# Expert slots of a mixture-of-experts layer: from one-hot matmuls to indirect writes into a table in memory

## The reference

```
x = layernorm(x + self_attention(x))              # 16 heads, low-rank latents, rotary part, causal
x = layernorm(x + cross_attention(x, ctx) @ W.T + b)   # 16 heads
p = softmax(x @ Wg + bg)                          # 8 experts
top2, weights = top_k(p, 2) renormalised to 1
y = sum over the 2 chosen experts e: weight_e * (gelu(x @ W1[e] + b1[e]) @ W2[e] + b2[e])
out = layernorm(x + y)
```

## Time and profile before

| | us |
|---|---|
| median of 3 runs | 707.59 (707.23 to 709.61) |
| span of the profiled execution (the page gives no other time of its own for it) | 704.8 |
| PE busy | 610.6 (87%) |
| DVE busy | 517.4 (73%) |
| ACT busy | 397.3 (56%) |
| POOL busy | 292.9 (42%) |

### The profile page before, as it was taken

The page is one execution under the profiler, slowest core; times in us unless marked ns, Lnnn a source line. Parts: engine busy times, 40 slices in busy tenths (PEclk is TensorE's granted clock), DMA queues, the critical chain, the costliest instruction groups (busy, mean ns, idle before and its releaser), DMA issues.

```text
span 704.8 us, 22698 instructions
## 1 busy us (share of the span) xinstructions
PE 610.6 (87%) x8063; PEld 447.7 (64%) x8064; DVE 517.4 (73%) x1106; ACT 397.3 (56%) x847; POOL 292.9 (42%) x245
## 2 busy tenths in 40 slices
PE   2678989999999999999886797899999999999940
PEld 1456756676676667667564556678777777777720
DVE  5797898997786878677677986867666666666635
ACT  4335668767568484866778693554434444444414
POOL 3688574436264641543111012233444444444422
PEclk9789999999999999999999997999999999999985
DMA  8435253240322304304344045122222222222226
GB/s 276 151 103 151 78 166 91 63 121 6 111 69 72 82 1 119 110 21 118 106 121 136 1 119 180 19 32 46 47 47 45 45 45 45 44 45 39 43 40 223
DMA packets 39839, 59.45 MB, mean 84 GB/s; under 512 B 6768, under 2 KB 27504, under 8 KB 39632
## 3 DMA queue, kind: packets, MB, share of 16 engines
q1 hardware_dynamic: 32272, 48.12, 23.3%
q0 software_dynamic: 7488, 10.23, 8.9%
HBM read 34.08 MB, written 11.67 MB: 65 GB/s over the span
## 4 chain that ended last, share of the span: by engine, by line
PE 34%; DVE 11%; DMA 6%; ACT 4%; issue 4%; POOL 2%; ACTq 1%; SPq 1%; DVEq 1%; POOLq 0%
PE bank L1688 6%; PE bank L1690 3%; DVE mxc L1085 3%; DMA x_sb<-x_rows,slot_row 2%; PE scores L1678 2%; PE bank L1678 2%; PE scores L1680 2%; PE scores L1679 2%; PE bank L1292 2%; DMA acc_rows<-x,slot_row 2%; PE bank L1680 2%; PE bank L1679 2%; POOL acc_rows L627 1%; ACT probs L742 1%; PE scores L1343 1%
## 5 line engine op out<-in xcount | busy, mean ns | idle before, releaser
L742 ACT ACTIVATE probs<-scores 128x768 f32<-128x768 f32 (+1 forms) x128 | 114.3, 918 | 51.0 <-PE scores L1349 40.2
L627 POOL DMA_INDIRECT acc_rows<-x,slot_row x39 | 65.2, 1671 | 132.7 <-DVE x L1198 129.8
L1688 PE MATMUL bank<-w_sb,wp 128*128 x312 | 109.9, 380 | 1.9 <-DVE wp L1185 1.9
L1085 DVE TENSOR_REDUCE mxc<-scores 128x4 f32<-128x1024 f32 x64 | 76.5, 1217 | 20.4 <-PE scores L1363 19.8
L1690 PE MATMUL bank<-w_sb,wp 128*128 x312 | 85.1, 273 | 0.0
L813 ACT ACTIVATE probs<-scores,b_sb 128x128 f32<-128x128 f32 x160 | 45.5, 368 | 63.3 <-PE scores L1680 63.3
L813 ACT ACTIVATE probs<-bank,b_sb 128x128 f32<-128x128 f32 x152 | 43.4, 370 | 65.6 <-PE bank L1680 65.6
L1183 DVE CAST wp<-probs 128x512 f16<-128x512 f32 x78 | 36.1, 462 | 60.3 <-ACT probs L813 59.8
L1050 DVE TENSOR_REDUCE mx<-scores 128x6 f32<-128x768 f32 x64 | 59.8, 950 | 15.7 <-PE scores L1331 15.2
L1678 PE MATMUL scores<-xT,w_sb 128*128 128x128 f16 x320 | 61.2, 223 | 2.2 <-DVE xT L909 1.2
L1679 PE MATMUL scores<-xT,w_sb 128*128 128x128 f16 x320 | 61.2, 223 | 0.0
(11 more groups left out here) (267 smaller groups left out, 1712.1 us busy)
## 6 DMA issues: line engine op xcount, KB each, us to landing
w_sb<-w_sb SPq DMA_DIRECT2D x192, 64.0 KB, 2.4
wstage<-in_w_exp SPq DMA_DIRECT2D x16, 512.0 KB
w_sb<-in_w_exp SPq DMA_DIRECT2D x8, 512.0 KB, 5.3
wp<-in_w_exp SPq DMA_DIRECT2D x8, 512.0 KB, 4.2
x_sb<-in_x_by_feature SPq DMA_DIRECT2D x8, 256.0 KB, 3.5
ctx_raw<-in_ctx SPq DMA_DIRECT2D x8, 256.0 KB, 3.1
x_res<-in_x SPq DMA_DIRECT2D x8, 256.0 KB, 3.5
x_rows<-x SPq DMA_DIRECT2D x8, 256.0 KB, 3.1
```

Of the source, the lines that this page charges most:

```text
L627: nc.gpsimd.indirect_dma_start(out=acc_rows[:, :], out_offset=bass.IndirectOffsetOnAxis(ap=slot_row[:, n:n + 1], axis=0), in_=yb[n % 2], i ...
L742: nc.scalar.activation(probs[:, 2 * (k % 4):2 * (k % 4) + 2, 0:cols], ps_p[pair[u, k, b]][:, :, 0:cols], ACT.Exp, scale=(SELF_SCALE, CROSS ...
L1085: nc.vector.tensor_reduce(mxc[:, 2 * k:2 * k + 2, :], ps_p[pair[u, k, b]][:, :, :].rearrange("p h (a k) -> p h a k", a=2), axis=AX.X, op=A ...
L1688: mm(o[:, 0:2 * D], ah[:, u, f, :], weights(e, at, 2 * D), start=(f == 0), stop=(f == FC - 1), skip_group_check=True)
```

## The change

The one-hot matrices and their matmuls are gone. A table in memory (`slot_table`, 16384 rows of 2 floats, 8 bytes each; row = 2048 * expert + rank) is filled with zeros at the start by SP. `gate_slots` on DVE computes the row number and casts it to an integer. For each block of 128 tokens and each of the two choices POOL issues one indirect DMA that writes 128 entries of 8 bytes (`put_slot`): 20 for the first group, 12 for the late one. When all have landed POOL loads the whole table back, 128 KB, in one DMA (`load_slots`), and `gate_table` reads that. DVE's `gate_late_tiles` stands in three parts behind tiles 1, 2 and 3, where it was one block behind tile 4.

```diff
 GPSIMD_ORDER
-cr.5 cx.7 sr.7 ss.7 ke.7 cr.6 gg.4 cr.7
+cr.5 cx.7 sr.7 ss.7 gp0.4 gp1.4 gp2.4 ke.7 cr.6 gp3.4 gp4.4 gl.4 gg.4 cr.7
...
+                        sp.dma_start(slot_table_rows, oP[0][:, 0, :]).then_inc(z_st, 16)
...
+            def put_slot(t, c):
+                nc.gpsimd.indirect_dma_start(
+                    out=slot_table[:, :], out_offset=bass.IndirectOffsetOnAxis(ap=slot_at[:, c, t:t + 1], axis=0),
+                    in_=slot_entry[:, t, c, :], in_offset=None).then_inc(t_st, 16)
+
+            def load_slots(g, t1):
+                pool.wait_ge(t_st, 32 * t1)
+                nc.gpsimd.dma_start(slots_seen[g].rearrange("p l a -> p (l a)"), slot_table_rows).then_inc(t_ld[g], 16)
...
+                elif u == "gate_put":
+                    if k == 0:
+                        pool.wait_ge(z_st, 48)
+                        pool.wait_ge(v_key, 1)
+                    for t in (2 * k, 2 * k + 1):
+                        for c in range(2):
+                            put_slot(t, c)
+                elif u == "gate_load":
+                    pool.wait_ge(a_cv, B)
+                    pool.wait_ge(p_cl, B)
+                    load_slots(0, SEEN * TT)
...
                 if n and n + AHEAD - 1 < N_TILES:
                     gather(n + AHEAD - 1)
+                if n == 0:
+                    pool.wait_ge(v_key, 2)
+                for t in range(3 * n, 3 * n + 3):
+                    if t < 2 * (NT - SEEN * TT):
+                        put_slot(SEEN * TT + t // 2, t % 2)
+                if n == 4:
+                    load_slots(1, NT)
                 scatter(n)
...
 def gate_slots
-                link(nc.vector.tensor_scalar(exps[:, at, :], rank, 1.0 / P, 0.5 / P - 0.5, ALU.mult, ALU.add))
-                link(nc.vector.tensor_scalar(exps[:, at, :], exps[:, at, :], 1.5 * 2.0 ** 23, None, ALU.add))
...
+                link(nc.vector.tensor_tensor(exps[:, at, :], rank, tab[:, C_EROW:C_EROW + E].unsqueeze(1).broadcast_to([P, n, E]), ALU.add))
+                link(nc.vector.tensor_tensor(picked[:, :, at, :], onehot[:, :, at, :],
+                                             exps[:, at, :].unsqueeze(1).broadcast_to([P, 2, n, E]), ALU.mult))
+                link(nc.vector.tensor_reduce(rs1[:, 0:2, at], picked[:, :, at, :], axis=AX.X, op=ALU.add))
+                nc.vector.tensor_copy(slot_at[:, :, at], rs1[:, 0:2, at]).then_inc(v_key, 1)
...
-            def gate_table(g, slots, i0, i1):
-                pe.wait_ge(v_S, SEEN + g)
+            def gate_table(g, i0, i1):
+                pe.wait_ge(t_ld[g], 16)
                 pe.wait_ge(v_sel, g + 1)
```

More of the change, by code:

```diff
@@ L59 @@
 C_EP = C_DUMMY + 1
-C_E16 = C_EP + E
-C_RP = C_E16 + E
+C_EROW = C_EP + E
+C_RP = C_EROW + E
 C_ALL = C_RP + 1
@@ L210, in decoder_layer @@
 def decoder_layer(nc, x, ctx_in, w_kv, g_kv, w_q, wq_content, wq_rope, wk_content, wk_rope, wv, wo, wx,
-                  x_by_feature, xb, wg, bg, w_exp, b1t, b2, table, masks, out, x2_rows, acc_rows):
+                  x_by_feature, xb, wg, bg, w_exp, b1t, b2, table, masks, out, x2_rows, acc_rows, slot_table):
     stack = ExitStack()
@@ L315, in decoder_layer @@
         onehot, picked = [xT_flat[1][:, i * 2 * NT * E:(i + 1) * 2 * NT * E].rearrange("p (k t e) -> p k t e", k=2, e=E) for i in range(2)]
[L316 to L319, removed]
+        slot_entry = swaps[:, 0:4 * NT].rearrange("p (t c a) -> p t c a", c=2, a=2)
+        slot_at = swaps[:, 4 * NT:6 * NT].bitcast(I32).rearrange("p (c t) -> p c t", c=2)
+        slots_seen = [ctx_raw[:, i, :].rearrange("p (l a) -> p l a", a=2) for i in range(2)]
         flat = oT[:, :, :].rearrange("p c t -> p (c t)")
@@ L662, in gate_exp @@
                 nc.scalar.activation(exps[:, t0:t1, :], shift[:, t0:t1, :], ACT.Exp).then_inc(a_re, 1)
[L664 to L671, removed]
             done = Counter()
@@ L950, in gate_slots @@
[L950 to L959, removed]
@@ L1383, in gate_ranks @@
                 last.then_inc(pe_rank, 1)
-            def gate_scatter(g, t, first, last=None):
-                pe.wait_ge(a_oh, t + 1)
-                for c in range(2):
-                    mm(ps_slots[g], oh_lane[:, t % 2, c, :], oh_vals[:, t % 2, c, :, :].rearrange("p a l -> p (a l)"),
-                       start=(t == first and c == 0), stop=(t == (last or first + 1) and c == 1)).then_inc(pe_slot, 1)
-            def gate_table(g, slots, i0, i1):
-                pe.wait_ge(v_S, SEEN + g)
+            def gate_table(g, i0, i1):
+                pe.wait_ge(t_ld[g], 16)
                 pe.wait_ge(v_sel, g + 1)
                 for i in range(2):
-                    last = mm(ps_fin[g][:, i * (i1 - i0):(i + 1) * (i1 - i0)], slots_of(slots, i), slot_t[2][:, i0:i1], start=True, stop=True)
+                    last = mm(ps_fin[g][:, i * (i1 - i0):(i + 1) * (i1 - i0)], slots_seen[g][:, :, i], slot_t[2][:, i0:i1], start=True, stop=True)
                 last.then_inc(pe_fin, 1)
-            def slots_of(slots, i):
-                return slots[:, i * P:(i + 1) * P]
             at, covered = Counter(), {}
@@ L1457, in bank3_free @@
                 once(v_key, at["gate_ranks"])
-                once(v_S, at["gate_scatter"])
                 once(v_lg, at["logits"])
@@ L1479, in _ @@
                     bank1_free()
-                    once(t_ld, 32)
+                    once(tab_ld, 32)
                     pe.wait_ge(v_kvn, b + 1)
@@ L1740, in _ @@
                     gate_ranks(*GATE[1])
-                elif n in (2, 3, 4):
-                    for t in range(GATE[1][1] + 2 * (n - 2), GATE[1][1] + 2 * (n - 1)):
-                        gate_scatter(1, t, GATE[1][1], NT - 1)
                 elif n == 6:
-                    gate_table(1, slots_all, FIRST, N_TILES)
+                    gate_table(1, FIRST, N_TILES)
             with pe.Fori(0, (N_TILES - 2 - FIRST) // 2) as j:
```

114 lines of the change are left out of this document (41 added, 73 removed), and 4 rows, old and new, of the table UNITS.

## The result

The changed kernel takes 727.31 us, median of 4 runs (726.4 to 731.04), against 708.3 of the kernel before: ratio 1.0286 [1.0249, 1.0323]. Its profiled span is 724.9 us against 704.8, that is +20.1. Forecast were 707.6 and a range up to 723.

What follows compares the result with a forecast made beforehand. It took the chain at the end of attention and, in the expert phase, PE with POOL's gather queue behind it as bounds; 4.2 - 1.2 - 3.2 + 0.2 = 0.0 left the span at 704.8, forecast 707.6 us, range 701 to 723.

Steps and rivals of the forecast that it cites:

- The puts on POOL: POOL's indirect writes of table entries: 1.4 us each with the gap, bounds 1.25 and 1.93.
- Dear puts: Rival: a put costs as much as the accumulating scatter, 1.63 + 0.30 to issue; 723.5 us, slower; chance 0.23.
- puts held by DVE: Rival: DVE's five weight pieces each hold a put under way, table 6 us late; 713.6 us, slower; chance 0.12.
- The rule on the shared port pair: A DMA issued from GpSimd waits until DVE's instruction ends; by the rows 0.2 us a put.
- The +3.3 us up to the selection: End of attention: PE's table selection starts at 426.3 instead of 423.01, behind puts, landing and load.
- 12 puts and then keep: POOL, first group: 12 puts from 389.5 end at 406.3; keep and root follow, waiting for nothing.
- Last put to load: End of attention: the last put, issued at 419.3, lands 3.4 us later, at 422.7; bounds 2.8 and 4.4.
- The clock: PE idle some 7 us before the selection, so low clock: projection takes twice 1.97 us, selection 0.4 more; +1.9 us.
- One-hots removed in attention: 40 records of PE matmuls and 20 comparisons go, ahead of the table selection; counted as nothing.
- the -1.2 for the wait: Expert phase: late gate_slots halves and PE's 1.20 us wait for DVE's xT at 447.91 goes; -1.2 us.
- the -1.0 for the clock: Tile 0: the low clock stretch begins earlier and may end before the tile does; between 0 and -2.7 us.
- -3.2 for slots 3 to 8: Expert phase: one-hot matmuls go, POOL gets three puts an iteration; 33.2 us from slots 3 to 8 against 36.45.

Runs made afterwards that it cites:

- f3: Changed kernel with its 32 indirect stores made plain, to consecutive rows, and its two loads reading a constant table: ratio 0.9916 to the kernel before.
- h1: Changed kernel with plain stores in attention (20), indirect ones in the expert phase (12), loads reading a constant table: ratio 1.0039.
- b3: Kernel before plus 8-byte indirect stores that nobody needs, 6 and 4 in two runs at the end of attention: ratio 1.0163.
- c2: Changed kernel with each store waiting until the last but one before it has landed, at most two under way: 739.2 us, ratio 1.0481.
- h2: Kernel before plus 20 indirect 8-byte stores, one in each of tiles 13 to 32 behind the gather, nobody waiting: ratio 1.0085.
- f2: Kernel before with its 39 gathers and 39 scatters as plain loads and stores, the scatters' adding left out: ratio 0.9961.
- d3: Kernel before plus 12 indirect 8-byte stores in the expert phase, three behind each of gathers 3 to 6, nobody waiting: ratio 1.0139.
- the run with gathers: Kernel before plus 20 indirect gathers of 8 bytes at the changed kernel's store places, results unused: ratio 1.0266.
- b1: Kernel before plus 20 indirect 8-byte stores, one at a time between other POOL operations from batch 2 to batch 5 of attention: ratio 1.0234.

## Why the prediction was wrong

**The puts on POOL.** Right, and a little cheap: 1.26 to 1.48 us from start to start within a run, mostly 1.27 (1.4 taken). "Dear puts" (from 1.6 us a put on) is out, and so is "puts held by DVE": none of 32 took over 1.174 us. The rule on the shared port pair (the Trainium skill, SBUF — State Buffer, SBUF: two separate sides) would have shown as longer puts; the longest is 0.2 us over the median.

**The step that failed** is the assumption under every term: that a put costs what POOL spends on it, and what queues behind it. I counted POOL's row and not what a call does to the others. Of the rivals the price of "dear puts" (723.5 us) came closest, by another mechanism; that is luck. The +3.3 us up to the selection became +17.9:
- 12 puts and then keep: predicted at 406.3, was 413.18, **+6.9**. I wrote that keep waits for nothing; it waited 7.43 us for batch 6's residual. In f3, with plain puts and a granted clock as low as here (0.53 and 0.50 between 395 and 405 us; 0.50 in the changed kernel, 1.00 in the trace of before), keep came at 407.12. So 6.1 us go with the index, that is with PE's late completions (6.2 us at 406.29 in the changed kernel). The other 0.8 are there in f3 as well, where the projection of batch 6 takes 3.55 us at the low clock.
- keep, root and 8 puts: 12.4 us against 13.0 predicted, **-0.6**.
- Last put to load: 3.4 predicted, 11.8 measured, **+8.4**. The bounds of 2.8 and 4.4 came from gathers alone in their stretch. In f3, with plain puts, the load waited 4.45 us for the landing instead of 10.86.
- Load to selection: 3.55 against 3.4 and 0.1 to start, 0.

**The clock.** Right in kind and near in size: from the selection to tile 0 it took 12.8 us against 11.3, +1.4; predicted were +1.9, and -1.0 in tile 0 itself, behind its first matmul. The projection took 3.76 us instead of 1.97, and the windows after show a granted clock of 0.50 (1.2 GHz) where PE had waited 6.39 us for the table:

```profile
435.00:440.00 5.00, 0.00 (x0) 0.00 (x0) 0.00 (x0) 1.24 (x2) 0.59 (x1) 0.59 0.86 195
440.00:445.00 5.00, 4.06 (x12) 3.46 (x13) 1.38 (x3) 1.06 (x1) 2.20 (x2) 0.50 0.16 32
```

**One-hots removed in attention: nothing.** Right as far as f3 shows: tile 0 at 435.13 without them, 434.34 with them.

**Expert phase.** From tile 0 to slots 3 the -1.2 for the wait and the -1.0 for the clock were -1.8 together. But -3.2 for slots 3 to 8 was +3.6. With plain stores it is -6.3, so the gain from the removed one-hots was there and larger than I said, and 12 indexed calls turn it round (h1, 40.6 us). I had forecast that POOL's iterations would be the bound, 7.4 us without idle time. They were not:

```profile
477.88 1.60 POOL L648 DMA_INDIRECT acc_rows<-x,slot_row  x1 [2.67 <-DVE x L1186]
...
485.14 1.60 POOL L648 DMA_INDIRECT acc_rows<-x,slot_row  x1 [0.30 <-issue]
...
496.98 1.60 POOL L648 DMA_INDIRECT acc_rows<-x,slot_row  x1 [4.85 <-DVE x L1186]
```

Between these scatters lie 7.3 and 11.8 us, and POOL waits for DVE, that is for tiles which the same lateness holds up. The row of waits from 455 to 510 us (us in total, times, longest) shows it on ACT, which has no such wait in the trace of before:

```profile
ACT probs L829 <- remote: 17.8, 4, 6.4
```

**The whole.** f3 at 0.9916, h1 at 1.0039, the changed kernel at 1.0286: of the 26 us between f3 and the changed kernel about 9 belong to the 12 late calls and 17 to the 20 in attention. The sum that I made would have erred by 6 us for stores without an index, and it erred by 20 for these.

**What stays open.** What in an indexed call holds back PE's completions and other queues' landings. Excluded, at the end of attention, are bytes, direction, number of rows, scattered places and POOL's time; the reading of the index by POOL and what the DMA engines do with it were not told apart. The loss has two forms, and what links them is not shown: PE's signals come late beside runs of twelve and eight calls back to back and beside three an iteration; landings come late beside fewer calls too (b3, c2), and they cost time without any late signal. That calls cost little in the steady loop (h2, f2) fits a lateness that only hurts where an engine stands waiting for a signal, as in attention with its short hand-overs between PE, DVE and ACT; but h2's 6 us lie between that and a price for each, and its calls stand one to a tile where d3's stand three to a tile, so that the wider spacing can be the reason as well: this is argued and not shown. No version here beats both kernels and computes the same: f3's gain needs stores that know their rows beforehand.

## What to carry to other kernels

Price an added transfer by what it does to the others, not by its row on the engine that issues it: add a few copies of it that nobody waits for to the old kernel and time that. It costs one run and would have settled this change. Here an indirect DMA more cost the whole kernel 0.6 to 1.2 us in a stretch with tight hand-overs between engines, with 16 rows as with 128, and 0.3 in a steady loop at one to a tile, while plain DMAs from POOL cost at most 0.1; so make few indexed calls, and keep them out of such stretches. A wait of "remote", or an idle time of "issue" in the middle of a group, beside POOL's DMAs is a sign of it; a trace without one is no proof of the contrary (b3 and c2), so look at the landings of the other queues too.

## What the runs showed of the hardware that I had not expected

- Completions of PE came 5.6 and 8.2 us behind the modelled end of their matmuls, with later matmuls already issued (402.85 and 427.05 in the run with gathers). Of the 20 traces only those with indexed calls back to back, twelve and eight or three an iteration, have signals over 0.65 us late.
- 64 KB moves on SP's queue landed in a median 4.1 us instead of 2.0 with four indexed calls among them (b1), and 512 KB of weights took some 12 us instead of 5 (b3).
- A put of 128 entries of 8 bytes takes POOL 0.97 us, but the last of the 20 to land took 11.8 us or more. The Trainium skill (DMA: Bandwidth & Descriptors, Specifications) says that transfers below 512 bytes are read, modified and written; 8, 64 and 512 bytes cost 1.0, 0.8 and 0.8 us each with overlapping intervals, and 8 bytes without an index 0.1, so that rule is not what decided here.
- A plain DMA of the same 128 entries takes POOL 0.54 us, and 12 of them 6.68 us in a row.
